# Embedding stage: additions of pixel pairs done by accumulating transfers, and the tap powers spread over eight groups

## The reference

```python
xf = fft.rfft2(xp, norm='ortho').real          # xp: 196 patches of 16x16 in each of 64 images, 3 channels
xf = xf * freq_weight_h[:, None] * freq_weight_w[None, :]
x_proj = xf.reshape(B, N, C*P*PW) @ proj_w.T + proj_b
h = concatenate([cls, x_proj], 1) + position_embeddings      # 64 x 197 x 192, float32
h = h + ssm_convolution(layernorm(h))          # one filter of 197 taps per channel, from 64 complex states each
h = h + moe_ffn(layernorm(h))                  # a shared expert and the two best of eight experts
```

## Time and profile before

| | us |
|---|---|
| three runs, median (lowest to highest) | 1329.42 (1326.73 to 1336.03) |
| the profiled execution | 1326.68 |
| its span in the trace | 1324.9 |
| PE / DVE / ACT / POOL busy in the span | 1071.4 / 940.1 / 589.8 / 723.0 |

### The profile page before, as it was taken

How to read it: one execution, slowest core, us unless ns; L and a number is a source line. 1 busy time by engine, 2 the same in 40 slices (tenths; PEclk the granted TensorE clock), 3 DMA queues, 4 the chain that set the end, 5 groups by cost and what they waited for, 6 DMA issues and landing times. The chain is left out here.

```text
span 1324.9 us, 27607 instructions
## 1 busy us (share of the span) xinstructions
PE 1071.4 (81%) x8823; PEld 730.8 (55%) x8824; DVE 940.1 (71%) x2721; ACT 589.8 (45%) x1091; POOL 723.0 (55%) x762
## 2 busy tenths in 40 slices
PE   2685999576179999999999996888888788883997
PEld 2464877475146555566666664555555455552555
DVE  6999899221258888877777865577677667672898
ACT  1124556431245565555555542445455455451332
POOL 2337789100038777777776861265566556554643
PEclk9867999797689999999999998999999999996999
DMA  6445888699874443333333216333333333431997
GB/s 211 149 177 189 290 287 217 159 280 196 178 187 133 130 127 94 97 97 94 97 97 95 68 56 181 91 105 108 111 112 104 111 97 117 116 99 58 324 313 228
DMA packets 213258, 198.10 MB, mean 150 GB/s; under 512 B 69712, under 2 KB 192114, under 8 KB 212910
## 3 DMA queue, kind: packets, MB, share of 16 engines
q1 hardware_dynamic: 178936, 141.27, 38.2%
q0 software_dynamic: 19488, 39.17, 8.8%
q10 hardware_dynamic: 14742, 16.49, 5.3%
HBM read 123.58 MB, written 74.41 MB: 149 GB/s over the span
## 5 line engine op out<-in xcount | busy, mean ns | idle before, releaser
L1166 POOL DMA_INDIRECT routed<-rows_w,slot x198 | 215.0, 1086 | 68.1 <-issue 67.9
L1604 POOL DMA_INDIRECT parts<-unit_yu,unit_token x208 | 206.5, 993 | 76.0 <-issue 75.7
L424 PE MATMUL ps<-w_hi,xh 128*98 128x192 f16 x384 | 106.9, 278 | 49.0 <-POOL xl L346 49.0
L1348 DVE SCALAR_TENSOR_TENSOR hf<-psu,sg 128x512 f32<-128x512 f32 x120 | 82.8, 690 | 84.0 <-ACT sg L1089 38.3
L1016 PE MATMUL pso<-ffn_w_hi,hh 128*128 128x192 f16 x480 | 119.2, 248 | 27.9 <-DVE hl L1353 21.7
L1089 ACT ACTIVATE sg<-psg 128x512 f32<-128x512 f32 x120 | 71.9, 599 | 147.3 <-PE psg L1001 114.2
L346 POOL TENSOR_TENSOR xl<-area,xh 128x784 f16<-128x784 f32 x48 | 89.6, 1894 | 74.3 <-ACT xh L293 74.3
L1001 PE MATMUL psg<-xt,ffn_w_hi 128*128 128x512 f16 x360 | 119.3, 386 | 0.0
L1016 PE MATMUL pso<-ffn_w_hi,hl 128*128 128x192 f16 x480 | 119.0, 248 | 0.2 <-issue 0.2
L1016 PE MATMUL pso<-ffn_w_lo,hh 128*128 128x192 f16 x480 | 119.0, 248 | 0.0
L1001 PE MATMUL psu<-xt,ffn_w_hi 128*128 128x512 f16 x360 | 117.3, 380 | 0.0
(11 more groups left out here) (237 smaller groups left out, 3162.2 us busy)
## 6 DMA issues: line engine op xcount, KB each, us to landing
unit_xu<-routed SPq DMA_DIRECT2D x53, 392.0 KB
area<-in_xa_dram SPq DMA_DIRECT2D x48, 392.0 KB, 4.7
area<-in_xb_dram SPq DMA_DIRECT2D x48, 392.0 KB, 5.9
end_part<-parts SPq DMA_DIRECT2D x48, 384.0 KB, 5.6
toeplitz<-taps SPq DMA_DIRECT2D x24, 600.2 KB
resid<-h ACTq DMA_DIRECT2D x32, 294.0 KB
hin<-resid SPq DMA_DIRECT2D x24, 384.0 KB
yin<-mixed SPq DMA_DIRECT2D x96, 96.0 KB
```

Of the source, the lines that this page charges most:

```text
L424: nc.tensor.matmul(out, xh[i][:, c, t], w_hi[:, c], start=(c == 0), stop=False)
L1166: nc.gpsimd.indirect_dma_start(out=routed[:, :], out_offset=bass.IndirectOffsetOnAxis(ap=slot[q][:, k, t:t + 1], axis=0), in_=rows_w[q][:, ...
L1348: nc.vector.scalar_tensor_tensor(out=hf[i][:], in0=psu[:, i], scalar=1.0 / SCALE, in1=sg[i][:], op0=ALU.mult, op1=ALU.mult).then_inc(s["hf ...
L1604: nc.gpsimd.indirect_dma_start(out=parts[:, :], out_offset=bass.IndirectOffsetOnAxis(ap=token[q][:, k:k + 1], axis=0), in_=y[q][:, k, :], ...
```

## The change

Five things. (1) `xb` is no longer loaded into slots of its own: POOL issues transfers that read xb from memory and add it to xa in `area` (`accum_op=ALU.add`), three per group, in `fold(g)`, which POOL issues two groups ahead of `low(g)`, behind a wait for the group's xa. (2) All of `area` now holds slots of xa, NSLOT = 12, four groups. (3) DVE's additions are gone; ACT waits for all three additions of a group. The semaphores x_in and folded are now one for each of four groups. (4) The chain of powers has eight pieces (steps 0 to 7), and the tap products go with groups 8 to 13 (KG = 8). (5) Some waits of DVE for its own results (hc, add) now go through the common counter, and crs shares cve's semaphore.

```diff
--- before.py
+++ after.py
@@ -39,7 +39,7 @@
 GT = GI * NPATCH
 ROWS = 128
 NX = 18
-NSLOT = 6
+NSLOT = 12
 QG, RQ = 4, 32
 
 
@@ -51,7 +51,7 @@
 DQ = DH // 2
 SKIP = KL - SEQ
 RW = SKIP + 1 + HALF + TC
-AREA = max(2 * NSLOT * GT, NPATCH * DQ)
+AREA = max(NSLOT * GT, NPATCH * DQ)
 
 
 NTOK = B * SEQ
@@ -124,15 +124,12 @@
 
 def pixel_slots(area):
 
-    at = [area[:, n * GT:(n + 1) * GT] for n in range(2 * NSLOT)]
-    return at[0::2], at[1::2]
+    return [area[:, n * GT:(n + 1) * GT] for n in range(NSLOT)]
 
 
 def load_pixels(sp, io, x_in, area, g, c):
-    xa, xb = pixel_slots(area)
     n = C * g + c
-    for dst, src in ((xa, "xa"), (xb, "xb")):
-        sp.dma_start(dst[n % NSLOT], io[src][g, :, c]).then_inc(x_in[n % NSLOT], 16)
+    sp.dma_start(pixel_slots(area)[n % NSLOT], io["xa"][g, :, c]).then_inc(x_in[g % QG], 16)
 
 
 def pieces_of(region, shapes):
@@ -187,7 +184,7 @@
         k0 = sb("k0", [1, D])
         yc = sb("yc", [1, D])
 
-        xa, xb = pixel_slots(area)
+        xa = pixel_slots(area)
         xe = [sb(f"xe{i}", [ROWS, GT]) for i in range(2)]
         xh = [sb(f"xh{i}", [ROWS, C, GT], F16) for i in range(2)]
         xl = [sb(f"xl{i}", [ROWS, C, GT], F16) for i in range(2)]
@@ -210,15 +207,16 @@
         psk = [ps[0:CG * KA, i * GI:(i + 1) * GI, 2 * D:2 * D + CG * KB] for i in range(2)]
 
         names = ("loaded_w", "loaded_a", "loaded_c", "pos_in", "pws_ready", "wps_ready", "whi_ready", "w_ready",
-                 "hc_ready", "cmv_ready", "cve_ready", "crs_ready", "uc_ready", "vector_done", "powers_ready",
+                 "cmv_ready", "cve_ready", "uc_ready", "vector_done", "powers_ready",
                  "kf_ready", "zero_ready", "taps_out", "k0_in", "yc_ready", "out_done",
-                 "add_ready", "folded", "xh_ready", "xl_ready", "eh_ready", "es_ready", "tokens_ready",
+                 "xh_ready", "xl_ready", "eh_ready", "es_ready", "tokens_ready",
                  "h_ready", "stats_ready", "mv_ready", "ve_ready", "rs_ready", "mr_ready", "nb_ready", "const_ready",
                  "u_ready", "h_out0", "h_out1")
         s = {name: sem(name) for name in names}
-        x_in = [sem(f"x_in{i}") for i in range(NSLOT)]
+        x_in = [sem(f"x_in{i}") for i in range(QG)]
+        folded = [sem(f"folded{i}") for i in range(QG)]
         e_in = [sem(f"e_in{i}") for i in range(2)]
-        KG, NK = 5, NCG // GI
+        KG, NK = 8, NCG // GI
         block = ctx.enter_context(nc.Block())
 
         @block.sync
@@ -245,9 +243,11 @@
             for n in range(C):
                 load_pixels(sp, io, x_in, area, 0, n)
             load_rest(0)
-            for n in range(C, NSLOT):
+            for n in range(C, 2 * C):
                 load_pixels(sp, io, x_in, area, n // C, n % C)
             load_rest(1)
+            for n in range(2 * C, NSLOT):
+                load_pixels(sp, io, x_in, area, n // C, n % C)
             sp.wait_ge(s["zero_ready"], 1)
             for n in range(2):
                 sp.dma_start(taps[n * DH:(n + 1) * DH, KL:RW], zero[:]).then_inc(s["taps_out"], 16)
@@ -287,7 +287,7 @@
             def split(g):
                 for c in range(C):
                     n = C * g + c
-                    act.wait_ge(s["folded"], n + 1)
+                    act.wait_ge(folded[g % QG], 16 * C * (g // QG + 1))
                     if g >= 2 and c == 0:
                         act.wait_ge(s["tokens_ready"], GI * (g - 1))
                     nc.scalar.copy(xh[g % 2][:, c], xa[n % NSLOT][:]).then_inc(s["xh_ready"], 1)
@@ -339,6 +339,12 @@
 
         @block.gpsimd
         def _(pool):
+            def fold(g):
+                pool.wait_ge(x_in[g % QG], 16 * C * (g // QG + 1))
+                for c in range(C):
+                    n = C * g + c
+                    pool.dma_start(xa[n % NSLOT], io["xb"][g, :, c], accum_op=ALU.add).then_inc(folded[g % QG], 16)
+
             def low(g):
                 for c in range(C):
                     n = C * g + c
@@ -371,11 +377,15 @@
             pool.wait_ge(s["cmv_ready"], 1)
             nc.gpsimd.tensor_scalar(cve[:], cmv[:, 1:2], EPS, None, ALU.add).then_inc(s["cve_ready"], 1)
             pool.wait_ge(s["cve_ready"], 1)
-            nc.gpsimd.tensor_tensor(crs[:], cve[:], mhalf[0:3, 0], ALU.pow).then_inc(s["crs_ready"], 1)
-
+            nc.gpsimd.tensor_tensor(crs[:], cve[:], mhalf[0:3, 0], ALU.pow).then_inc(s["cve_ready"], 1)
+
+            fold(0)
+            fold(1)
             for step in range(NG + 3):
                 if 0 <= step - 3 < NG:
                     rstd(step - 3)
+                if step + 2 < NG:
+                    fold(step + 2)
                 if step < NG:
                     low(step)
 
@@ -504,45 +514,43 @@
 
                 if at == 0:
                     cmul(t1, v, p)
-                    for _ in range(4):
+                    for _ in range(2):
+                        twice(t1, t1)
+                if at == 1:
+                    for _ in range(2):
                         twice(t1, t1)
                     coefficients()
-                if at == 1:
+                if at == 2:
                     twice(t2, t1)
                     twice(t4, t2)
                     twice(t8, t4)
+                if at == 3:
                     both(ta, t8, t4)
                     both(t14, ta, t2)
                     step(nc.vector.tensor_scalar(t14[:, 1], t14[:, 1], -1.0, None, ALU.mult))
-                if at == 2:
                     nc.vector.memset(zq[:, 0, 0], 1.0)
                     nc.vector.memset(zq[:, 1, 0], 0.0)
                     for m, t in ((1, t1), (2, t2), (4, t4), (8, t8)):
                         power(zq, m, t)
+                if at == 4:
                     raised(zq, 3, zq[:, :, 2], 1, 1)
                     raised(zq, 5, zq[:, :, 4], 1, 3)
                     raised(zq, 9, zq[:, :, 8], 1, 5)
-                if at == 3:
+                if at == 5:
                     power(tb.unsqueeze(2), 0, t14)
                     raised(zp, 1, tb, 0, 1)
                     twice(t1, t14)
                     power(tb.unsqueeze(2), 0, t1)
                     raised(zp, 2, tb, 0, 2)
+                if at == 6:
                     twice(t2, t1)
                     power(tb.unsqueeze(2), 0, t2)
                     raised(zp, 4, tb, 0, 4)
-                if at == 4:
+                if at == 7:
                     twice(t4, t2)
                     power(tb.unsqueeze(2), 0, t4)
                     raised(zp, 8, tb, 0, 7)
                     dve.sem_inc(s["powers_ready"], 1)
-
-            def fold(g):
-                for c in range(C):
-                    n = C * g + c
-                    dve.wait_ge(x_in[n % NSLOT], 32 * (n // NSLOT + 1))
-                    nc.vector.tensor_tensor(xa[n % NSLOT][:], xa[n % NSLOT][:], xb[n % NSLOT][:],
-                                            ALU.add).then_inc(s["folded"], 1)
 
             def low_rows(m):
                 dve.wait_ge(s["eh_ready"], m + 1)
@@ -591,12 +599,11 @@
                                     ALU.mult).then_inc(s["pws_ready"], 1)
 
             dve.wait_ge(s["loaded_c"], 32)
-            nc.vector.tensor_tensor(hc[:], cl[:, 0], cl[:, 1], ALU.add).then_inc(s["hc_ready"], 1)
-            dve.wait_ge(s["hc_ready"], 1)
+            tt(hc[:], cl[:, 0], cl[:, 1], ALU.add)
             step(nc.vector.bn_stats(cst[:], hc[:]))
             nc.vector.bn_aggr(cmv[:], cst[:]).then_inc(s["cmv_ready"], 1)
             dve.wait_ge(s["pos_in"], 32)
-            nc.vector.tensor_tensor(add[:], add[:], pos[:], ALU.add).then_inc(s["add_ready"], 1)
+            tt(add[:], add[:], pos[:], ALU.add)
             for k in range(order - 1, 4, -1):
                 taylor(k)
 
@@ -608,14 +615,12 @@
                                            op0=ALU.mult, op1=ALU.add).then_inc(s["w_ready"], 1)
             for k in range(4, 1, -1):
                 taylor(k)
-            dve.wait_ge(s["crs_ready"], 1)
+            dve.wait_ge(s["cve_ready"], 2)
             nc.vector.tensor_scalar(uc[:], hc[:], cmv[:, 0:1], crs[:], ALU.subtract, ALU.mult
                                     ).then_inc(s["uc_ready"], 1)
-            dve.wait_ge(s["add_ready"], 1)
 
             for at in range(NG + 2):
                 if at < NG:
-                    fold(at)
                     if at % QG == 0:
                         low_rows(at // QG)
                 if 0 <= at - 2:
```

## The result

The changed kernel took 1350.87 us in the median of 4 runs (1345.85 to 1362.23), the kernel before, beside it, 1332.03 (1326.73 to 1336.03): a ratio of 1.0156, 95% interval 1.008 to 1.0232. It is slower by 1.6%, where 15 us less were forecast. The profiled execution has a span of 1343.7 us against 1324.9. Of these 18.8 us, 14.9 lie in the first stage: the next stage's first load starts at 263.88 instead of 248.96 us. The other 3.9 us lie somewhere in the later stages, whose code is the same; they weren't looked into.

The account below looks back on a forecast made before the run. DVE was taken to bound the first five groups, PE the rest. Chain's end 126 us, plus 92 (218), plus 4 for transfers: last product 222 instead of 239, 2 given back; 1326.7 - 15 = 1312 us, range 1298 to 1350.

Parts of the forecast that it names:

- What bounds the kernel: First stage, the embedding: DVE sets the pace of the first five groups, PE the rest, with POOL close behind.
- 84 was the sum: DVE's own work from 25.6 us to the eighth chain piece's end: chain 53, closings 29, two low_rows of 1.0 us.
- The lock, 16 us of a range from 0 to 34: Port lock between POOL's xl and DVE's chain: 4.2 us per group where they meet, 16 us taken, eighth piece ending at 126.
- PE's 84 and POOL's 92 us for the last eight groups: Groups after the chain: PE needs 84 us, POOL 8 x 11.5 = 92 us, so last products end at 218 us.
- The transfers: Accumulating transfers in the first stage: twice a plain one's cost, 4 us over POOL's 218, last product at 222 us.
- The issue, 1.35 us: Each transfer issue on POOL costs 1.35 us, as for a later stage's indirect issues; 4.05 us per group.
- The end of the stage, 2 us: After the last product, the taps' rows are written later and yc becomes late: 2 us added.
- The low end of the range, 1298: Free lock and cheap transfers: PE's 84 us from 115 us on, giving 1298 us.
- The first: Rival, chance 0.20: lock and transfers take what DVE frees; eighth piece ends at 144 us, 1326 us in all.
- The second: Rival, chance 0.18: accumulating transfers are the bound from a factor of about 2.5 on; 1348 us, at factor 3 1376.
- the third: Rival, chance 0.07: POOL's issuing is the bound; at 2.7 us an issue the period is 15.5 us, 1369 us in all.

Follow-up runs that it names:

- h_first: The changed kernel with POOL's order xl, issues, rstd in each step; ratio to the kernel before 1.0212.
- g_behind: The changed kernel with POOL's three issues for group g+2 placed behind xl(g) instead of ahead of it; ratio to the kernel before 1.0011.
- b_chain8: The kernel before with the chain in eight pieces and tap products behind groups 8 to 13, DVE still adding; ratio to the kernel before 0.9965.
- d_plain: The changed kernel with xl on DVE and plain transfers for the accumulating ones (sum left out), executed once; last products at 237.2 us.
- d_lowdve: The changed kernel with xl computed by DVE instead of POOL, behind each closing; ratio to the kernel before 0.9937.

## Why the prediction was wrong

By its own steps:

- *What bounds the kernel.* Right: DVE up to the chain's end, then PE. DVE's own work there was 131 - 54 = 77 us; 84 was the sum, 7 too many.
- *The lock, 16 us of a range from 0 to 34.* This is the step that failed, by 38 us (54 measured), and it alone exceeds the whole error (the last products at 254 instead of 222 us). Both factors were wrong. How many runs meet the chain: about four of eight were assumed, "since xl(g+2) runs as soon as PE is through with g, which is about when DVE begins a closing"; it was eight of the nine runs until then: the first three find no closing to run under, for the next four rstd's wait, ahead of xl in the queue, ties the run to the closing's *end*, the eighth meets a closing, and the ninth follows without a wait. The prediction named what is queued behind the wait for xa, but not what is queued behind the wait for DVE. h_first, in which most runs fall under closings, loses 16.7 us. And the price of one: 4.2 us, three operations held in turn, as in the first chain stretch; it was 4.8 to 4.9 for a run directly behind rstd (g_behind) and 6.2 in the mean with issues ahead, so the upper end should have been 8 x 6.2 = 50 us and not 34. The error at the last products is smaller, 32 us, since the 7 us too many of DVE's own work and the 4 us for the transfers stand against it.
- *A part that wasn't seen.* The additions on DVE did more than cost 2.75 us. xl waited for them, and so ran under the closing, which it doesn't hold up (its four additions took 1.95 us beside xl, and 1.95 us in the changed kernel at 70.21 us, with no xl beside them). Taking them away moved xl. b_chain8 has the additions and loses 11 us, the changed kernel 54.
- *PE's 84 and POOL's 92 us for the last eight groups.* 254 - 160 = 94: the right total by luck. POOL needs 10.1, not 11.5 us per group, so PE sets the pace (11.07 us), and the rest is group 8 at a granted clock of 0.53.
- *The transfers.* The factor of 2 was right (2.0). Whether the 4 us that I took for them were needed stays open: d_plain, which could have shown it, ran at a lower granted clock. They are not what made the change slower: g_behind and d_lowdve make the same transfers, and their stages end 16 and 25 us earlier.
- *The issue, 1.35 us.* 0.90 us of POOL's time each.
- *The end of the stage, 2 us.* 0.5 us.
- *The low end of the range, 1298.* The sum doesn't give it: PE's 84 us from 115 us on end at 199, 40 us before 239, and with the 2 us at the end that is 1289.
- *The rivals.* The first named the mechanism, with the Trainium skill's rule (page "SBUF — State Buffer", section "Who interferes with whom": the pair of ports is an exclusive lock that the first taker keeps for a whole instruction), and priced it at 34 us: 1326. The trace goes beyond the rule: the hold lasted not one instruction but a run of three, and the issues in it. The second and the third didn't come about: the DMA share was 1.08 in the early stretch, but transfers were not what ended last behind it, and an issue took 0.90 us.

## What to carry to other kernels

An instruction that is taken away may have set the time at which others start. Before pricing a shared resource by "half of the cases", follow each user of it back to what releases it: a wait that stands ahead of it in the same in-order queue, or in that of the engine that feeds it, decides where it falls, and if the other engine's own work gives that release, the two can meet every time. And where two engines hold each other out, a run of long instructions on one can cost the other nearly the whole run, whether it holds one operation throughout or one per instruction (4.8 to 4.9 and 4.2 to 4.4 us of 4.9 here). Give the run to one of the two (xl on DVE: 25 us less here), let it fall where the other isn't held (b_chain8), or keep the issues from ahead of it (g_behind: 16 us less).

## What was unexpected of the hardware

- One DVE operation of 0.26 us took 6.61 us, held through three POOL instructions of 1.65 us and part of the issues ahead. In g_behind, where POOL's run began after an idle wait, DVE had three operations in the same time (1.7 us each).
- An accumulating transfer of 392 KB takes 2.22 us of the 16 engines against 1.15 for the plain one, and its issue 0.90 us of POOL's time against 0.56.
- After similar chain ends (134 and 130 us), PE had a granted clock of 0.93 in one kernel and 0.64 in the single execution of another that had less transfer traffic, which cost 9 us.
